# All loads of A issued by ScalarE's queue, five of them ahead of its first work, in a graph layer with split float32 operands

## The reference, cut to what matters

```
# x: (1354, 512) float32, adj: (1354, 1354) float32 (normalised, sparse in values, stored dense)
h = max(layernorm(x), 0)                    # per row of 512, eps 1e-5
S = (adj + adj.T) * 0.5 + I
deg = sum(S, axis=1); dinv = deg ** -0.5 where deg > 0, else 0
L = dinv[:, None] * S * dinv[None, :]
out = x + (adj @ L) @ h
```

## Time and profile before

| | us |
|---|---|
| median of 3 runs | 177.32 |
| lowest, highest | 176.56, 177.72 |
| the profiled execution | 177.11 |
| its span | 175.20 |

### The profile page before, as it was taken

How to read it: one execution, slowest core, us unless ns; L and a number is a source line. 1 busy time by engine, 2 the same in 40 slices (tenths; PEclk the granted TensorE clock), 3 DMA queues, 4 the chain that set the end, 5 groups by cost and what they waited for, 6 DMA issues and landing times.

```text
span 175.2 us, 2027 instructions
## 1 busy us (share of the span) xinstructions
PE 161.5 (92%) x736; PEld 138.3 (79%) x736; DVE 84.9 (48%) x153; ACT 80.8 (46%) x156; POOL 30.2 (17%) x55
## 2 busy tenths in 40 slices
PE   0059999999999999999999999999999999999993
PEld 0048888888888888886788888888888889999992
DVE  0567678888876976955054041226312225400121
ACT  2778789999977994904235222122221222200000
POOL 1237945653055710000000000000000000000000
PEclk9999999999999999999999999999999999999999
DMA  5999999988996000000013930002300000500112
GB/s 178 402 417 414 401 412 406 372 320 295 351 308 156 4 0 0 0 0 0 4 35 80 424 129 0 2 4 82 137 0 0 0 4 18 201 0 0 53 49 98
DMA packets 8023, 25.20 MB, mean 144 GB/s; under 512 B 867, under 2 KB 2659, under 8 KB 8013
## 3 DMA queue, kind: packets, MB, share of 16 engines
q1 hardware_dynamic: 7581, 24.38, 37.8%
q10 hardware_dynamic: 432, 0.69, 1.2%
HBM read 22.14 MB, written 2.77 MB: 142 GB/s over the span
## 4 chain that ended last, share of the span: by engine, by line
PE 92%; DMA 3%; DVE 2%; POOL 1%; issue 1%; ACT 0%; SPq 0%; POOLq 0%; DVEq 0%
PE bank L541 47%; PE bank L577 45%; DMA AT<-in_adj_t_dram 3%; DVE S L390 1%; ACT g L323 0%; POOL power L249 0%; DVE y_out L491 0%; POOL S L240 0%; SPq L194 0%; DVE g_scale L424 0%; DVE base L399 0%; DVE part_sums L395 0%; DVEq L389 0%; POOLq L248 0%; POOLq L232 0%
## 5 line engine op out<-in xcount | busy, mean ns | idle before, releaser
L541 PE MATMUL bank<-g,ring 128*128 128x512 f32 (+1 forms) x352 | 82.9, 398 | 10.7 <-ACT g L323 10.7
L541 PEld LDWEIGHTS bank<-g,ring 128*128 128x128 f32 (+1 forms) x352 | 66.1, 188 | 27.1 <-issue 10.7
L577 PE MATMUL bank<-ring,z 128*128 128x468 f32 (+1 forms) x384 | 78.8, 367 | 0.0
L577 PEld LDWEIGHTS bank<-ring,z 128*128 128x128 f32 x384 | 72.2, 188 | 6.5
L335 ACT CAST ring<-AT 128x468 fp32r<-128x468 f32 (+1 forms) x33 | 18.2, 569 | 43.6 <-PE bank L577 43.6
L473 DVE TENSOR_TENSOR ring<-AT,ring 128x468 fp32r<-128x468 f32 (+1 forms) x30 | 18.2, 625 | 34.2 <-ACT ring L335 28.0
L408 DVE SCALAR_TENSOR_TENSOR S<-S,AT 128x1354 f32<-128x1354 f32 (+1 forms) x11 | 17.2, 1561 | 0.8 <-POOL S L240 0.8
L429 DVE TENSOR_TENSOR ring<-S,ring 128x1024 fp32r<-128x1024 f32 x10 | 12.3, 1226 | 6.8 <-ACT ring L312 6.8
L491 DVE TENSOR_TENSOR y_out<-bank,x_res 128x468 f32<-128x468 f32 (+1 forms) x12 | 7.0, 622 | 16.9 <-PE bank L577 16.9
L340 ACT ACTIVATE z<-bank,d_scale 128x512 fp32r<-128x512 f32 (+1 forms) x12 | 7.4, 691 | 14.1 <-PE bank L541 14.1
L312 ACT CAST ring<-S 128x1024 fp32r<-128x1024 f32 x11 | 11.4, 1035 | 1.0 <-DVE S L390 0.6
(11 more groups left out here) (42 smaller groups left out, 36.0 us busy)
## 6 DMA issues: line engine op xcount, KB each, us to landing
AT<-in_adj_t_dram SPq DMA_DIRECT2D x10, 677.0 KB, 6.6
S<-in_adj_dram SPq DMA_DIRECT2D x10, 677.0 KB, 8.5
x_in<-in_x_dram SPq DMA_DIRECT2D x11, 256.0 KB, 5.6
x_res<-in_x_t_dram SPq DMA_DIRECT2D x1, 2708.0 KB, 9.3
out_dram<-y_out SPq DMA_DIRECT2D x8, 234.0 KB, 2.2
out_dram<-y_out SPq DMA_DIRECT2D x4, 209.0 KB, 1.9
S<-in_adj_dram ACTq DMA_DIRECT2D x2, 256.0 KB, 4.4
AT<-in_adj_t_dram SPq DMA_DIRECT2D x2, 256.0 KB, 4.9
```

The lines of the kernel that those rows point to most:

```text
L541: return nc.tensor.matmul(dst, stationary, rhs[0:r, parts[1], :], start=first, stop=final)
L577: last = nc.tensor.matmul(out_bank(span, j), z[0:r, k, parts[0], j * P:(j + 1) * P], both[0:r, parts[1], 0:w], start=k == 0 and parts == ( ...
```

## The change

ACT issues all loads of A. A1 to A5, for which the ring has room, go out right behind the three pieces of A0, ahead of ACT's first computation. A6 to A11 are issued in ACT's loop, each in round n = b - 5 after copy_hi(n), with the same waits on `rests` and `hi_copied` that SP had. SP keeps x, A.T, x transposed and the stores, in the same order, without those two waits.

```diff
@@ block.sync
                 fetch_x(b)
                 sp.dma_start(AT[0:r, b, :], AT_in[b * P:b * P + r, :]).then_inc(load_row[b - 1], 16)
-                if b >= AROWS:
-                    sp.wait_ge(rests, b - AROWS + 1)
-                    sp.wait_ge(hi_copied, b - AROWS + 1)
-                sp.dma_start(S[0:r, b % AROWS, :], A[b * P:b * P + r, :]).then_inc(load_row[b - 1], 16)
@@ block.scalar
+            def fetch_row(b):
+                r = rows_of(b)
+                if b >= AROWS:
+                    act.wait_ge(rests, b - AROWS + 1)
+                    act.wait_ge(hi_copied, b - AROWS + 1)
+                act.dma_start(S[0:r, b % AROWS, :], A[b * P:b * P + r, :]).then_inc(load_row[b - 1], 16)
...
             for j, (c0, c1) in enumerate(FIRST_CUTS):
                 act.dma_start(S[:, 0, c0:c1], A[0:P, c0:c1]).then_inc(load_first[j], 16)
+            for b in range(1, AROWS):
+                fetch_row(b)
             x_moments(0)
...
             for n in range(1, FULL):
                 head_row(n)
                 copy_hi(n)
+                if n + AROWS - 1 <= NB:
+                    fetch_row(n + AROWS - 1)
                 x_moments(n + 1)
                 scale_g(n)
                 x_centre(n + 1)
```

## The result

The changed kernel takes 181.21 us (median of 4 runs, 180.98 to 181.43), beside 177.52 us for the kernel before (4 runs, 176.56 to 177.79). The ratio is 1.0217, with a 95% interval of 1.018 to 1.0255: slower by 3.7 us. With its fourth run the kernel before has a median 0.2 us above the 177.32 of the table ahead of the prediction. The profiled execution took 180.98 us with a span of 179.1.

The account below looks back on a forecast made before the run. TensorE, which never waits once started, was taken as the bound; holes do not add, so only step 2's +4.4 us counted: 177.11 profiled gave 181.5, plus 0.2 to the median 181.7 us; range 178.8 to 183.8.

Parts of the forecast that it names:

- TensorE has no slack, so only its starts count: TensorE never waits after starting at 10.73 us, so only its start and later holes move the end.
- The queues alternate by packet: DMA engines alternate between SP's and ScalarE's queues by packet, not byte; each tile SP moves lets one of A through.
- Row 0, +1.4 us: A.T0's third piece, paired with A1, lands at 9.3 us; TensorE starts at 12.15; bounds 0 to +1.7.
- ScalarE's own delay is covered: Five issues before ScalarE's first work delay its first sum by 1.1 us; cost 0, uncovered at most 1.1.
- Row 1: POOL's diagonal of row 1 comes 3.4 us later, g's head at 20.5, a 0.8 us hole before step 1.
- Rows 2 and 3: A.T2 and A.T3 land behind more tiles of A; TensorE's step 2 starts at 28.2 instead of 23.8, +4.4 us.
- the second route: Row 3's load, complete at 24.8 us, sets POOL's diagonal of row 3; the other route, the masks, gave 24.9.
- The issues in the loop are covered: A6 to A11 add 0.43 us each to ScalarE's loop; cost 0, without cover at most 1.2 us.
- Rival A: The DMA engines share by bytes: step 2 at 25.4, +1.6 us, 178.9 us; chance 0.12.
- C: A's early tiles fill only gaps SP's queue leaves, so nothing is lost: 177.3 us; chance 0.08.
- Rival B: TensorE's clock drops in the holes, a second set of slow matmuls costing 1.8 us: 183.5 us; chance 0.12.
- the prediction's last term: From the start of POOL's diagonal of row 3 to the end of g's head of row 2: 3.3 us.

Follow-up runs that it names:

- experiment 4: Changed kernel with each row of A1 to A11 moved as two packets of 2,708 B instead of one of 5,416 B: 177.61 us, ratio 1.0036.
- Experiment 2: Kernel before plus eleven tiny DMAs on ScalarE's queue where the changed kernel issues A: 177.25 us, ratio 1.0012.
- Experiment 5: Changed kernel with POOL's tail masks moved ahead of its first diagonal: 180.79 us, ratio 1.0242.
- experiment 1: Kernel before, all loads but A0 on SP's queue, written in the order two alternating queues should give: 181.61 us, ratio 1.0243.

## Why the prediction was right

The forecast of 181.7 us was 0.5 above the 181.2 measured, inside the range, and the mechanism is the one it named. As a growth it was 0.7 too large (4.4 forecast, 3.7 measured); the median of the kernel before came out 0.2 higher, which hides a part of that. Step by step:

- *TensorE has no slack, so only its starts count.* Right. Step 2 came 3.82 us late and the span grew by 3.9.
- *The queues alternate by packet.* Right: 170 packets to 161 with 0.62 MB to 0.21, 16 to 16 in one round, and experiment 4 moved the share by the packet's size alone.
- *Row 0, +1.4 us.* Too large; +0.9 was measured (11.63 against 10.73). The third piece of A.T0 landed at 2.16 + 6.6 = 8.8 us, not 9.3, so A1 cost it 1.1 us and not a full tile of 1.7. The packets of the piece began from 5.98 to 7.12 us before and from 6.05 to 8.04 us after. The queues in these two stretches, before and after:

```profile
q1 hardware_dynamic: 258, 0.39, 90.7%
q10 hardware_dynamic: 69, 0.07, 17.6%
...
q10 hardware_dynamic: 171, 0.66, 81.0%
q1 hardware_dynamic: 160, 0.20, 27.5%
```

ScalarE's queue moved 0.59 MB more in it, most of a tile, so the pairing was as forecast. But SP's queue moved 0.19 MB less: before, the stretch also held packets that weren't of the piece, mostly of x1. The net 0.40 MB are 1.0 us at 408 GB/s. The sum had taken the piece as if it had had the engines to itself before.
- *ScalarE's own delay is covered.* Right in the cost. Its first sum began at 6.12 (5.8 expected), the head of row 0 ended at 9.6 (9.4 expected), and g waited longer still. Experiment 2 shows the cover alone, and experiment 4 where it ends.
- *Row 1.* A.T1 landed at 3.16 + 11.3 = 14.5 us (15.06 forecast), and step 1 started at 20.08 (20.5).
- *Rows 2 and 3.* A.T2 landed at 20.2 (20.7). The diagonal of row 3 came at 24.93 (24.9), through the masks, and the load of row 3 at 9.08 + 15.5 = 24.6 (24.8). Experiment 5 confirms the second route. From that diagonal to the end of g's head I took the 3.3 us of before; it took 26.74 + 0.72 - 24.93 = 2.5, since the diagonal itself ran 0.41 us instead of 1.18. That 0.8 is the term that was too large: with step 2 at 27.6 instead of 28.2 the 4.4 us were 3.8. The diagonal had run beside VectorE's remainder of the row before, and came just behind it after, as the last section shows.
- *The issues in the loop are covered.* Right. There is no hole after step 2, and g of row 3 was ready at 31.34 + 0.72 = 32.1, a full 1.0 us before step 3 wanted it at 33.1.

```profile
31.34 0.72 ACT L326 ACTIVATE g<-xr,g_scale 128x512 fp32r<-128x512 f32 x1 [0.25 <-DVE g_scale L431]
```

- *Rival A* (share by bytes) and *C* (nothing lost) are gone. *Rival B*, the clock, didn't happen in the changed kernel, but it was no idle thought, as the last section shows.

The Trainium skill's sentence in "DMA: Bandwidth & Descriptors", section "Issuing engines are not separate DMA queues", holds here: the second queue brought no bandwidth (409 against 408 GB/s). What decided the time is told in the same page's section "Queues, rings and completion order" of the Trainium skill: an engine goes round its queues packet by packet. The page's packet isn't the profile's, though: it is a group of typically 9 to 17 descriptors, while the turns in this trace are of one row (16 packets of each queue in 0.28 us on 16 engines), and here the measurement decides. The runs add that a queue with longer packets gets more of the bytes.

## What to carry to other kernels

When the DMA engines are full, a load that is issued early is paid for by the loads that are needed now; spreading loads over two queues changed who was served first here, and not the rate. The two queues shared by packets, so the queue of 5.4 KB rows took bytes from the one that had 2 KB rows between its tiles. A prefetch on a queue of its own takes its turns at once, whether its tile is wanted yet or not. Before moving a load, count the bytes that will stand ahead of the tile the pipeline needs next, and look for an order on another engine (here powers behind the next row's diagonal) that ties one row to the load of the next.

## What was not expected

**The clock fell after a hole of experiment 1.** In experiment 1 the first hole was about 2.3 us (a window of 2.56, in which the last matmul of step 0 still ran for 0.39), longer than any in the changed kernel. Its windows on TensorE (columns as above):

```profile
14.90:17.90 3.00, 3.00 (x15) 1.00 1.02 418
17.90:20.46 2.56, 0.39 (x2) 1.00 1.04 416
20.46:21.60 1.14, 1.14 (x5) 1.00 1.01 408
21.60:25.10 3.50, 3.50 (x11) 0.51 1.02 401
25.10:27.90 2.80, 2.69 (x12) 1.00 1.01 414
```

TensorE came back at full speed for 5 matmuls, and then the granted clock was 0.51, the 1.2 GHz level, for 3.5 us with 11 matmuls instead of 15. The second hole swallowed this, as step 2 had to wait anyway: two more of this kernel's four runs had a mean clock of 0.991 and one had 1.000, and their times, 181.58 to 181.87 us, don't tell them apart. One of the four runs of experiment 5 had a mean clock of 0.991 and took 182.7 us where the others took 180.7 to 180.8. Its own rows weren't taken, so that its clock fell behind a hole isn't shown; the 1.9 us would fit the 1.8 that rival B had for it. The changed kernel, with holes of 0.6 and 2.0 us, was granted 0.997 or more in all four runs.

**POOL's instructions ran long beside VectorE.** The first of the masks in the changed kernel, and at the start in experiment 5:

```profile
21.12 1.34 POOL L255 TENSOR_SCALAR_AFFINE_SELECT eye_x<-eye_x 128x74 f32<-128x74 f32 x1
```

```profile
1.96 0.25 POOL L255 TENSOR_SCALAR_AFFINE_SELECT eye_x<-eye_x 128x74 f32<-128x74 f32 x1
```

The same instruction took 1.34 us beside VectorE's sum of a row (20.79 to 22.36) and 0.25 us at 1.96 us, before VectorE had begun. All the masks together took some 4.3 us there and 1.7 us here. The diagonal of row 3 shows the same the other way round. VectorE's remainder of row 2 in the kernel before:

```profile
19.46 1.25 DVE L429 TENSOR_TENSOR ring<-S,ring 128x1024 fp32r<-128x1024 f32 x1 [0.47 <-ACT ring L312]
```

Before, the diagonal began at 19.80 in the midst of it and took 1.18 us. In the changed kernel that remainder ran from 23.48 to 24.71; the diagonal began at 24.93, 0.22 us behind it, and took 0.41. That is the 0.8 us by which the prediction's last term was too large. That VectorE is the cause is argued from these rows; no run changes VectorE's work alone.
